# A three-stage long-convolution layer with feed-forward: the projection run in two passes, with the first unit's preparation between the row tiles of the second

## What is computed

```python
xp = (einsum('btd,de->bte', X, Wp) + bp).reshape(B, T, 4, D)   # projection: y and three gates
f  = (pos @ Wf + bf).reshape(T, 3, D)                          # filters, pos = sine encoding
# both padded with zeros to 2T along time: a causal convolution through FFTs
y = xp[:, :, 0, :]
for i in range(3):
    conv = irfft(rfft(y, axis=1) * rfft(f)[None, :, i, :], n=2*T, axis=1)
    y = conv * xp[:, :, i + 1, :]
x = layernorm(X + y[:, :T])
x = layernorm(x + ffn(x))         # silu(x Wg) * (x Wu), then Wd, weights are int * 1/127
```

## Time and profile before

| | |
|---|---|
| median of 3 runs | 971.78 us (971.59 to 972.85) |
| profiled execution, its own time | 972.62 us |
| its span, first to last instruction | 970.4 us |
| mean granted TensorE clock | 0.969 |
| TensorE busy over the span | 876.6 us, 90% |
| VectorE, ScalarE, GpSimd busy | 767.4, 529.7, 645.3 us |
| DMA traffic | 155.16 MB, mean 160 GB/s |

### The profile page before, as it was taken

One profiled execution on the slowest core, in us unless ns is written; L12 is line 12 of the kernel. 1 busy time (PEld: TensorE's weight loads), 2 busy tenths in 40 slices (PEclk: granted clock), 3 DMA queues, 4 the chain that ended last, 5 costly groups with the idle time before them and its releaser, 6 DMA issues. The chain is left out here.

```text
span 970.4 us, 21584 instructions
## 1 busy us (share of the span) xinstructions
PE 876.6 (90%) x8204; PEld 678.0 (70%) x8204; DVE 767.4 (79%) x1318; ACT 529.7 (55%) x1048; POOL 645.3 (66%) x679
## 2 busy tenths in 40 slices
PE   3999999947999999999999999954899999999994
PEld 2888888846888888888888888732456556555563
DVE  2777777735899898888889889846688898988864
ACT  2253334446788888878887667314344444444441
POOL 2555555403888898898898889862676666667642
PEclk8999999969999999999999999996999999999998
DMA  5596556488566567566667877328123224222011
GB/s 205 192 348 214 188 173 205 165 230 238 164 189 174 165 194 197 174 179 175 193 195 213 262 235 209 109 105 276 45 66 120 77 65 130 65 77 74 23 45 44
DMA packets 165788, 155.16 MB, mean 160 GB/s; under 512 B 3457, under 2 KB 151937, under 8 KB 165313
## 3 DMA queue, kind: packets, MB, share of 16 engines
q1 hardware_dynamic: 164176, 145.24, 49.3%
q10 hardware_dynamic: 1520, 8.68, 2.3%
HBM read 111.18 MB, written 42.73 MB: 159 GB/s over the span
## 5 line engine op out<-in xcount | busy, mean ns | idle before, releaser
L564 POOL TENSOR_TENSOR gz<-prod 128x512 f32<-128x512 f32 x180 | 230.4, 1280 | 88.2 <-DVE prod L507 87.0
L507 DVE TENSOR_TENSOR prod<-bank,wfx 128x1024 f32<-128x1024 f32 x180 | 219.8, 1221 | 32.5 <-ACT bank L437 30.7
L396 PE MATMUL bank<-gz,ei 128*128 128x256 f32 x720 | 186.8, 382 | 2.2 <-POOL gz L564 2.0
L149 PE MATMUL bank<-wps,xs 128*128 128x512 f32 x768 | 176.4, 392 | 5.6 <-POOL xs L250 5.6
L149 PEld LDWEIGHTS bank<-wps,xs 128*128 128x128 f32 x768 | 145.6, 190 | 36.1 <-DVE wps L218 5.7
L939 POOL TENSOR_TENSOR hl<-hf,hh 128x512 f16<-128x512 f32 x96 | 111.8, 1173 | 82.4 <-ACT hh L793 82.4
L437 ACT COPY bank<-bank 128x512 f32<-128x512 f32 x180 | 102.8, 571 | 105.4 <-PE bank L344 105.4
L250 POOL TENSOR_TENSOR xs<-xt,xs 128x256 fp32r<-128x256 f32 x128 | 93.3, 752 | 97.4 <-ACT xs L181 97.4
L574 POOL TENSOR_TENSOR y<-y,gate 128x256 f32<-128x256 f32 x192 | 143.3, 747 | 5.1 <-DVE y L518 5.1
L344 PE MATMUL bank<-yh,ef 128*128 128x256 f16 x720 | 137.6, 273 | 2.3 <-ACT bank L437 1.3
L396 PEld LDWEIGHTS bank<-gz,ei 128*128 128x128 f32 x720 | 122.8, 190 | 15.8 <-POOL gz L564 6.5
(11 more groups left out here) (77 smaller groups left out, 1960.2 us busy)
## 6 DMA issues: line engine op xcount, KB each, us to landing
toep<-filter_rows SPq DMA_DIRECT2D x48, 1024.0 KB, 7.1
gates<-staged SPq DMA_DIRECT2D x16, 1536.0 KB, 6.3
gate<-gates SPq DMA_DIRECT2D x48, 512.0 KB, 4.1
xt<-in_XT SPq DMA_DIRECT2D x16, 512.0 KB, 5.0
attn_out<-y SPq DMA_DIRECT2D x16, 512.0 KB, 5.5
ya<-attn_out SPq DMA_DIRECT2D x16, 512.0 KB, 4.6
xr<-in_X SPq DMA_DIRECT2D x16, 512.0 KB, 5.4
out_x<-oo SPq DMA_DIRECT2D x16, 512.0 KB, 3.4
```

What stands on the lines that cost most here:

```text
L149: mm = pe.matmul(bank[n % 4 * 2 + half][:, :], xs[:, n % XSS, half, hx, k, :], wps[:, hw, k, half * 512:(half + 1) * 512], start=(k == 0 a ...
L396: mm = pe.matmul(dst, ei[:, h, e0 * P:(e0 + 1) * P], gz[:, n % 3, h, :], start=False, stop=(h == 1))
L507: nc.vector.tensor_tensor(prod[:, n % 2].rearrange("p r j (c b) -> p r j c b", b=NB), b_copy[n % 2][:, :].rearrange("p (r c b) -> p r c b" ...
L564: nc.gpsimd.tensor_tensor(gz[:, n % 3], prod[:, n % 2, 0], prod[:, n % 2, 1], ALU.add).then_inc(gz_ready, 1)
```

## The change

The projection runs as two passes over the 64 row tiles. The first pass takes only the reversed x and the first 512 columns (y and gate 2), the second only the straight x and the other 512 (gates 1 and 3). Each pass has 6 products for a row tile into one of `PBK` = 4 banks (banks 2 to 5); `XSS` is 4, and a slot holds one x part. Each x tile is loaded twice, 32 loads in all. The first pass stores 512 KB for a tile `a`, the second two times 512 KB. The weights are split in two halves. Stages 1 and 2 are one block, and the buffers of stage 1 lie in memory that the loop uses later (`wp` and `st` in `toep`, `xt` in `prod` and `gz`, `wf`, `ftmp` and `frow` in `yh` and `yl`).

The filter products come behind row tile 5 of the first pass, their split at tiles 7 and 8. The tables are issued by ScalarE at tile 12 (`ones` and `bfr` at tile 6). The sums of squares run in the first pass, the last of them behind its last row tile. In the second pass, TensorE's stream has `norm(0)` behind tile 1, `norm(1)` behind tile 3, a `toeplitz(0, q)` behind tiles 5, 11, ..., 47 and a `prefix(0, p)` behind tiles 12, 24, 36 and 48; ScalarE has `high(0, q)` at 2, 8, ... and `evacuate(0, q)` at 7, 13, ..., 49; VectorE has `low(0, q)` at 3, 9, .... Unit 0's filter quarters and the first of unit 1 all use slot 0 (`slot(s)`), because slots 1 and 2 hold the staging. The loop starts at `u = 0`.

The core of the diff:

```diff
-XSS = 3
+XSS = 4
+PBK = 4
+        def slot(s):
+            return 0 if s <= NSUB else (s - NSUB) % TSLOT
# SP
+                for m in range(2 * NA):
+                    p, a = m // NA, m % NA
+                    if m + XTS < 2 * NA:
+                        sp.wait_ge(x_lo, NB * (m + 1))
+                        load_x(m + XTS)
...
+                    if m == 8:
+                        sp.wait_ge(f_stored, 16)
+                        sp.wait_ge(wp_lo, 2)
+                        load_filter(0)
+                    if p == 1 and a in (3, 6, 9, 12):
+                        sp.wait_ge(toep_done, 2 * (a // 3))
+                        load_filter(a // 3)
+                    sp.wait_ge(proj_used, NB * (m + 1))
+                    if p == 0:
+                        sp.dma_start(gate_ap[NG:2 * NG, :, a].rearrange("g p w -> p g w"),
+                                     st[:, m % 2, 0]).then_inc(g_out[m % 2], 16)
+                    else:
+                        for s in range(2):
+                            sp.dma_start(gate_ap[2 * s * NG:(2 * s + 1) * NG, :, a].rearrange("g p w -> p g w"),
+                                         st[:, m % 2, s]).then_inc(g_out[m % 2], 16)
+                for q in range(4):
+                    if q == 0:
+                        sp.wait_ge(g_out[0], NA // 2 * 16 + 6 * 32)
+                        sp.wait_ge(g_out[1], NA // 2 * 16 + 6 * 32)
+                    if q == 3:
+                        sp.wait_ge(g_out[0], NA // 2 * 48)
+                        sp.wait_ge(g_out[1], NA // 2 * 48)
+                        load_filter(NSUB + 1)
+                        load_filter(NSUB + 2)
+                    load_gate(0, q)
-                for u in range(-1, NU):
+                for u in range(NU):
# TensorE
+                def project(n):
+                    p = n // NT
+                    pe.wait_ge(x_lo, n + 1)
+                    if n >= PBK:
+                        pe.wait_ge(proj_used, n - PBK + 1)
+                    for k in range(KT):
+                        for q, (hx, hw) in enumerate(((0, 0), (0, 1), (1, 0))):
+                            mm = pe.matmul(b_proj[n % PBK][:, :], xs[:, n % XSS, hx, k, :],
+                                           wps[:, hw, k, p * 512:(p + 1) * 512], ...)
+                    mm.then_inc(proj_done, 1)
...
+                for n in range(NT):
+                    project(NT + n)
+                    if n == 1:
+                        norm(0)
+                    if n == 3:
+                        pe.wait_ge(norm_sum, 1)
+                        norm(1)
+                    if n == 5:
+                        pe.wait_ge(f_tmp, 6)
+                    if n % 6 == 5 and n // 6 < NQ:
+                        toeplitz(0, n // 6, 0)
+                        toeplitz(0, n // 6, 1)
+                    if n % 12 == 0 and 1 <= n // 12 <= 4:
...
+                        prefix(0, n // 12 - 1, range(NE))
-                for u in range(-1, NU + 1):
+                for u in range(NU + 1):
# ScalarE
+                def split(n):
+                    m, b = n // NB, n % NB
+                    if b == 0:
+                        act.wait_ge(xt_in[m % XTS], (m // XTS + 1) * 16)
+                    if n >= XSS:
+                        act.wait_ge(proj_done, n - XSS + 1)
+                    src = xt[m % XTS][:, :, b, ::-1] if n < NT else xt[m % XTS][:, :, b, :]
+                    nc.scalar.activation(xs[:, n % XSS, 0], src, ACT.Copy).then_inc(x_hi, 1)
...
+                    if n % 8 == 7 and n >= 15:
+                        first_squares(n // 8 - 1)
+                first_squares(NSEG - 1)
+                act.wait_ge(wfx_ready, 12)
+                act.wait_ge(f_done, 6)
+                for n in range(NT):
+                    split(NT + n)
+                    if n % 6 == 2 and n // 6 < NQ:
+                        high(0, n // 6)
+                    if n % 6 == 1 and 1 <= n // 6 <= NQ:
+                        evacuate(0, n // 6 - 1)
+                act.wait_ge(f_rows, 6)
+                high(1, 0)
+                act.wait_ge(proj_used, 2 * NT)
```

More of the change, by code:

```diff
@@ L253, in program @@
         yh = sb("yh", [P, 2, NA, W], F16)
         yl = sb("yl", [P, 2, NA, W], F16)
-        total = sb("total", [P, 1])
+        with nc.sbuf_tensor("wps", [P, 2, KT, (NS + 1) * D], F32R) as wps:
+            pass
         gate = sb("gate", [P, NA, W])
@@ L292, in unscale, with loads, staged @@
             return iscl[:, u % 3:u % 3 + 1].bitcast(F32)
+        def slot(s):
+            return 0 if s <= NSUB else (s - NSUB) % TSLOT
+        def loads(s):
+            return 16 * sum(slot(e) == slot(s) for e in range(s + 1))
+        def staged(m):
+            return 16 * (m // 2 + 1)
         with nc.Block() as block:
@@ L301, in load_filter @@
                                   ap=[[2, P], [2 * NL, CS], [1, 2 * P]])
[L302 removed]
+                    sp.dma_start(toep[:, slot(s)], src).then_inc(toep_in[slot(s)], 16)
                 def load_gate(u, q):
                     sp.dma_start(gate[:, 4 * q:4 * q + 4], gate_ap[u, :, 4 * q:4 * q + 4]).then_inc(gate_in[q], 16)
[L307 to L309 removed]
@@ L353, in toeplitz @@
                         if q % 2 == 0:
-                            pe.wait_ge(toep_in[s % TSLOT], (s // TSLOT + 1) * 16)
+                            pe.wait_ge(toep_in[slot(s)], loads(s))
                         pe.wait_ge(yl_ready, m + 1)
@@ L431, in _, with weights, first_squares @@
             def _(act):
+                def split(n):
[6 more added lines that the diff above has]
+                    nc.scalar.activation(xs[:, n % XSS, 0], src, ACT.Copy).then_inc(x_hi, 1)
+                def weights(half):
+                    cols = slice(half * 512, (half + 1) * 512)
+                    nc.scalar.activation(wps[:, 0, :, cols], wp[:, :, cols], ACT.Copy).then_inc(wp_hi, 1)
+                def first_squares(s):
+                    act.wait_ge(proj_used, NB * (2 * s + 2))
+                    for g in range(NG):
+                        if NG * s + g:
+                            act.wait_ge(sq_done, NG * s + g)
+                        nc.scalar.activation(junk[:], y[:, g, 2 * s:2 * s + 2, :], ACT.Square,
+                                             accum_out=nrm[:, g, s:s + 1]).then_inc(sq_done, 1)
                 def copy(u, k):
@@ L467, in _ @@
+                for u in range(NU + 1):
                     for k in range(NA):
-                        if 0 <= u < NU and k < NE:
+                        if u < NU and k < NE:
                             copy(u, k)
-                        if k == 0 and 0 <= u < NU:
+                        if k == 0 and u < NU:
                             act.wait_ge(pv_ready, u + 1)
```

371 lines of the change are left out of this document (176 added, 195 removed).

## The result

The changed kernel takes 984.62 us (median of 4 runs, 983.16 to 985.69) against 972.1 us before (4 runs): a ratio of 1.0129, 95% interval 1.0113 to 1.0144. It is 1.3% slower; forecast was 968.6, 0.3% faster, with a range of 957 to 977. The profiled execution has a span of 982.8 us where it was 970.4.

What follows compares the result with a forecast made beforehand. TensorE was taken to pace projection and unit loop. Head, projection (176.4), waits and moved work summed to the first state matmul (the date) at 225.5 against 231.95, 6.4 earlier; less 3.2 at the loop's start: 968.6 us, range 957 to 977.

Steps and rivals of the forecast that it cites:

- The head: Time before TensorE's first projection matmul: no filter stands ahead and half the weights is split, so it starts at 10.5 us.
- (a): First pass: VectorE's first collect waits for the second half of the weights on ScalarE; TensorE waits 1.1 us.
- (b): First pass: six filter matmul pairs between projects cost 2.6 us; a split behind the filter casts costs 0.6.
- (c): First pass, after split 12: ScalarE's four table issues and twelve activations delay the next tile; TensorE waits 3.0 us.
- (d): First pass: table transfers slow SP's x loads in the DMA queues; 1.5 us, from 0 to 5.
- The seam: Between the passes: last squares precede the second pass's first split; TensorE idles 5.3 us, and the clock fall costs 2.7.
- Clock falls: Lower TensorE clock behind (c) and the three filter waits, of which some will come: 2 us (0 to 6.5).
- R2: Rival: every wait of 2 to 5 us drops TensorE's clock, 1.7 us a fall; 975.1 us, chance 0.12.
- The loop's start: Start of the unit loop: late first gate load and filter for unit 1's second quarter lose 3.2 us (0.7 to 6).
- R1: Rival: filters land in time, tables delay nothing, the clock does not fall between tiles; 957.6 us, chance 0.23.
- R4: Rival: the change buys nothing, with (c) at its upper end and the loop's start 1.5 worse; 971.8 us, chance 0.08.
- R3: Rival: DMA binds the second pass below 278 GB/s, adding 12.1 us; 980.7 us, chance 0.10.

Runs made afterwards that it cites:

- the waits mended: Changed kernel with filter load earlier, last squares later, tables spread, first weights half split first, loop's first transfers reordered: 948.45 us, ratio 0.9745.
- the seam: Changed kernel with the last squares behind split 67 instead of ahead of split 64, and norm, high, low and near-lag steps later: ratio 1.0041.
- the loop's transfers: Changed kernel with first gate load ahead of the last tile's stores and unit 1's second-quarter filter ahead of the other gate loads: ratio 1.0077.
- the kernel with filled waits: Changed kernel with ten extra unused matmuls ahead of each of the three near-lag blocks that wait for a filter: ratio 1.0094.

## Why the prediction was wrong

The waits were right and nearly every one stood where it was placed. What failed is the claim that the filter waits would mostly leave the clock alone, the size of three more terms, and 2.6 us that the sum did not have, all to one side. By the prediction's own steps:

- **The head**, 10.5, was 12.35. The bounds went to 12. The cause is not the weights, which landed after 4.9 us instead of 7.5:

```profile
toep<-in_WP ACTq DMA_DIRECT2D x1, 1024.0 KB, 4.9
```

```profile
9.30 0.72 ACT L385 ACTIVATE xs<-prod 128x256 fp32r<-128x256 f32 x2 [6.36 <-DMA prod<-in_XT]
...
9.93 1.04 ACT L389 ACTIVATE wps<-toep 128x1024 fp32r<-128x1024 f32 x1
...
11.01 1.29 DVE L500 TENSOR_TENSOR wps<-toep,wps 128x1024 fp32r<-128x1024 f32 x1 [9.29 <-ACT wps L389]
```

ScalarE's stream has the x splits ahead of the weights, and x landed at 9.3. I took the weights' date for the start and did not ask for the x load's. With the weights ahead of the splits the start was 10.76.
- **(a)** 1.1 was 1.36, **(b)** 2.6 was 2.6, its 0.6 did not show; **(c)** 3.0 was 1.8, since the four table issues took 2.2 us and not 3.3.
- **(d)** 1.5 was 4.5, the upper end of its range. VectorE's row above shows what was late: it was held 7.6 us by a store, not by an x load. The run with the tables spread shows the burst as the cause. While the tables ran, from 34 to 45 us, ScalarE's ring (q10) and SP's (q1) moved:

```profile
q10 hardware_dynamic: 478, 3.87, 83.8%
q1 hardware_dynamic: 397, 0.63, 18.0%
```

  The columns are packets, MB and share of the 16 engines' time. The numbers of packets are nearly equal, and q10 has 86% of the bytes. By the Trainium skill's rule on taking turns by the packet ("DMA: Bandwidth & Descriptors", "Queues, rings and completion order") the prediction had put that share at 87% and this wait at up to 5 us; the trace agrees with both.
- **The seam** 5.3 was 5.5, its clock 2.7 was 2.7 (2.75), the first `high` 2.7 was 2.4.
- **The filters** 7.5 were 7.9.
- **Clock falls, 2**, were 7.8: 2.7 behind (d) and three times 1.7. This is the step that failed most. The prediction had the right price (R2: 1.7 a fall) and held the wait of 2.5 us to be short enough against the 4.6 us gap of the earlier trace rows. It is not: all three filter waits brought the lower clock, in both profiles of this kernel, and filling them moved the date by 5.7. The Trainium skill, "TensorE: Matmul & The Clock Gate", "HAM oscillation — how this bites in real kernels", describes such a repeated fall behind waits for transfers of about 3 to 5 us. The trace agrees, and shows it behind waits of 2.56 to 2.73 us. R2, which had it so, had a chance of 0.12.
- **Left out of the sum**, 2.6. TensorE has no idle time beside the waits listed, so the rest lies in the matmuls. A wait costs more than its idle time: the last projection matmul before it is recorded at 0.39 us, where the next one of a row starts 0.23 behind it. That is 0.16 each, 8 times: 1.3. And the first projection matmul behind norm, filter, near-lag or prefix products holds the next one back:

```profile
170.89 0.48 PE L252 MATMUL bank<-wps,xs 128*128 128x512 f32 x1
171.21 0.62 PE L252 MATMUL bank<-wps,xs 128*128 128x512 f32 x2
```

  0.32 from start to start where 0.23 is usual, 0.09 each, 15 times: 1.3. The prediction priced the moved work by the products alone.
- **The loop's start**, 3.2, was 6.9 (6.5 and the twelve near-lag products, 0.35), more than the 6 us that the prediction named as a sign of being wrong. The 3.2 does not follow from the two parts given for it, 1.7 for the gate and 2 for the filter. The filter of unit 1's second quarter was issued only at 244.64, when the last store had landed, and held TensorE until 253.78, 15.6 us after the date and not 14. The wait of 3.6 us dropped the clock once more (1.4 us), which the prediction left out.

The errors before the loop add to 1.9 + 0.3 - 0.6 - 1.2 + 3.0 + 0.2 + 0.1 - 0.3 + 0.4 + 5.8 = 9.6, with 0.4 for the cold start (24 matmuls in 8.17 us where 5.44 would do, 2.7 for 2.3) and the 2.6 left out 12.6 of 12.7 us. R1 and R4 did not come, and R3, DMA binding the second pass, is refuted. The gain that the change was worth in itself was also there: with the waits mended the date is 27.7 us ahead of the old one, where the prediction without its waits, (c), (d), seam, `high`, filters and their clock (3.0 + 1.5 + 8.0 + 2.7 + 7.5 + 2), would give 200.8; measured was 203.9.

One cause ran through several terms: each was bounded alone, but a wait, the 0.16 us at its start and often the clock's fall behind it come together.

## What to carry to other kernels

When work is put between the steps of a stage that one engine paces, list for each engine what now stands ahead of the next step's feed (here squares, a table burst, an evacuation, an x load), and date the feed: every feed that is later than the lead of the buffers is a wait of the pacing engine. Price each such wait with the clock fall that may come behind it (here 1.4 to 2.7 us). Then move the late feeds forward; here five changes of order, with no work removed, turned +1.3% into -2.6%.

## What the runs showed of the hardware that was not expected

TensorE's clock fell from 2.4 to 1.2 GHz behind every one of the fifteen filter waits of 2.4 to 4.0 us ahead of the loop (the changed kernel twice, the seam, the tables and the loop's transfers), and each fall cost 1.5 to 1.7 us. But the length of the wait does not decide alone: the wait of 2.43 us that ended at 130.92, some 4 us behind the rise of the clock at the seam, and its like in six other runs (2.35 to 2.50), brought no fall, nor did the loop's wait of 1.63 us once it was shortened. And a wait of 1.85 us, which brought none at the same place in six other profiles (1.82 to 1.91), brought one in the second profile of the kernel with filled waits:

```profile
38.03 6.22 PE L252 MATMUL bank<-wps,xs 128*128 128x512 f32 x19 [1.85 <-POOL xs L654]
...
36.00:44.00 8.00, 6.15 (x20) 4.79 (x20) 3.76 (x8) 5.61 (x17) 4.27 (x6) 0.79 1.04 432
```

The same program had no fall there in its first profile. What tells these waits from each other was not tried.

The landing times of single transfers also spread more than expected: the first pass's stores took 3.2 us at the median and 14.5 at the most, beside 5 MB from the other queue, which had about as many packets as SP's in that time and six times the bytes (q10 and q1 above).
